# The last retention slot takes the first tile of windowed attention, and the last two retention sequences finish inside the attention slots

## The reference, cut to what matters

```python
# third block, per sequence, 8 heads of 32
qT, kT, vT = proj(Wq), proj(Wk), proj(Wv)
S = g * S + k_t[..., :, None] * v_t[..., None, :]
y_t = jnp.einsum('bhde,bhd->bhe', S, q_t)
out = (ys - mean) * rsqrt(var + EPS)        # mean and var of a head over the sequence
x = layernorm(x + (out * gn_weight + gn_bias) @ Wo.T)
# fourth block, per sequence (depth 2)
h = shift_token(x); q, k, v = split(h @ wqkv)
q, k = rotary_xpos(l2norm(q) * qs, l2norm(k) * ksc)
x = x + local_attention(q, k, v) @ wo       # window of 128 tokens
x = x + (a * gelu(g)) @ w2 + b2
```

## Time and profile before

| | us |
|---|---|
| median of 3 runs (lowest to highest) | 2498.15 (2495.32 to 2499.03) |
| the profiled execution's own time | 2491.8 |
| its span, first to last instruction | 2490.0 |
| PE busy | 2304.1 (93%) |
| DVE / ACT / POOL busy | 1629.3 / 1254.5 / 722.8 |
| mean granted clock of PE | 0.977 of full |

### The profile page before, as it was taken

One profiled execution on the slowest core, in us unless ns is written; L12 is line 12 of the kernel. 1 busy time (PEld: TensorE's weight loads), 2 busy tenths in 40 slices (PEclk: granted clock), 3 DMA queues, 4 the chain that ended last, 5 costly groups with the idle time before them and its releaser, 6 DMA issues.

```text
span 2490.0 us, 42715 instructions
## 1 busy us (share of the span) xinstructions
PE 2304.1 (93%) x16434; PEld 1358.5 (55%) x16434; DVE 1629.3 (65%) x4233; ACT 1254.5 (50%) x2822; POOL 722.8 (29%) x717
## 2 busy tenths in 40 slices
PE   5999999999999899986999999999999999999997
PEld 2333333333552577663656666666666666666664
DVE  5777777776530465654876766677667777777754
ACT  2655555556222352224665566556655655566540
POOL 2222322330120221213433333333333333333321
PEclk7999999999999899988999999999999999999999
DMA  9233333341349301000000000000001000000001
GB/s 296 89 104 102 105 100 110 112 123 43 145 176 420 154 28 67 27 18 28 6 5 2 6 6 5 1 5 31 14 1 52 7 14 19 21 5 22 20 21 37
DMA packets 71114, 158.72 MB, mean 64 GB/s; under 512 B 6352, under 2 KB 48448, under 8 KB 63328
## 3 DMA queue, kind: packets, MB, share of 16 engines
q1 hardware_dynamic: 68608, 146.81, 16.8%
q0 software_dynamic: 2304, 9.18, 1.6%
HBM read 116.65 MB, written 35.13 MB: 61 GB/s over the span
## 4 chain that ended last, share of the span: by engine, by line
PE 72%; DVE 15%; ACT 4%; DMA 3%; issue 2%; POOL 2%; SPq 1%; POOLq 0%; DVEq 0%; ACTq 0%
PE banks L1895 9%; PE banks L1873 6%; PE banks L1754 6%; PE banks L262 5%; PE banks L1768 4%; PE banks L225 4%; PE banks L238 4%; PE banks L1855 3%; PE banks L1798 3%; PE banks L311 2%; PE banks L292 2%; PE banks L1813 2%; DVE arena L2404 2%; DMA arena<-in_e_Wg 2%; PE banks L1780 2%
## 5 line engine op out<-in xcount | busy, mean ns | idle before, releaser
L466 DVE TENSOR_REDUCE arena<-banks 128x1 f32<-128x512 f32 x512 | 324.2, 683 | 113.7 <-PE banks L225 113.6
L381 ACT ACTIVATE arena<-banks 128x512 f32<-128x512 f32 x512 | 279.1, 595 | 164.1 <-PE banks L238 162.2
L1895 PE MATMUL banks<-arena 128*128 128x512 f32 x640 | 293.3, 595 | 6.3 <-DVE arena L2112 5.9
L1965 ACT ACTIVATE arena<-arena 128x256 f32<-128x256 f32 (+1 forms) x512 | 286.4, 562 | 3.5 <-DVE arena L2065 3.1
L2203 POOL TENSOR_TENSOR arena<-arena 128x512 f32<-128x512 f32 x128 | 162.6, 1271 | 401.7 <-DVE arena L2096 401.7
L1754 PE MATMUL banks<-arena 128*128 128x512 f32 x512 | 245.5, 603 | 5.7 <-DVE arena L2096 4.9
L225 PE MATMUL banks<-arena 96*128 96x512 bf16 x512 | 204.2, 401 | 16.6 <-DVE arena L466 12.0
L238 PE MATMUL banks<-arena 128*128 128x512 bf16 x512 | 194.1, 385 | 2.2 <-ACT arena L381 1.3
L2199 POOL TENSOR_TENSOR arena<-arena 128x16 f32<-128x16 f32 x64 | 187.4, 2929 | 5.3
L1895 PEld LDWEIGHTS banks<-arena 128*128 128x128 f32 x640 | 116.8, 190 | 131.6 <-issue 119.4
L1937 ACT ACTIVATE arena<-arena 128x256 f32<-128x256 f32 (+1 forms) x256 | 102.1, 471 | 154.6 <-DVE arena L2041 154.6
(11 more groups left out here) (300 smaller groups left out, 4363.1 us busy)
## 6 DMA issues: line engine op xcount, KB each, us to landing
arena<-in_e_W SPq DMA_DIRECT2D x32, 1024.0 KB, 12.3
arena<-stacks SPq DMA_DIRECT2D x64, 384.0 KB, 4.6
arena<-in_e_Wg SPq DMA_DIRECT2D x16, 1024.0 KB, 14.9
stacks<-arena SPq DMA_DIRECT2D x32, 384.0 KB, 2.5
stacks<-arena SPq DMA_DIRECT2D x32, 256.0 KB, 2.7
arena<-dens POOLq DMA_DIRECT2D x32, 256.0 KB, 4.6
arena<-in_xT SPq DMA_DIRECT2D x8, 512.0 KB, 9.0
stacks<-arena SPq DMA_DIRECT2D x32, 128.0 KB, 2.5
```

The source lines that it names most:

```text
L381: e.activation(ex[:, j], self.psum[:, self.exp_bank1(k)], ACT.Exp).then_inc(s["a_e"], 1)
L466: e.tensor_reduce(mx[:, t, j:j + 1], self.psum[:, k % 3], AX.X, ALU.max, negate=True).then_inc(s["a_m"], 1)
L1895: i = e.matmul(bank, weights[:, c], self.hT[:, c], start=c == 0, stop=c == 1)
L1965: k = e.activation(pr[:, h, at:], pr[:, h, at:], ACT.Exp, bias=mx[:, h:h + 1], scale=rn[:, h:h + 1], accum_out=den[:, h:h + 1])
```

## The change

Slots 9 and 10 of retention and slot 0 of the fourth block are gone as slots of their own. What they held is spread out. The last retention slot (`*3_last`, sequence 7's products) now also has tile 0's projection, squares, lengths, rotation, scaling and values. Slot 1 of the fourth block also has sequence 7's coefficients, head scaling, output product and addition, and sequence 6's statistics and norm. Slot 2 also has the turn of sequence 6 and the statistics, norm and turn of sequence 7. No instruction is added or removed other than waits. `Ring` banks of the last turns are fixed by hand (banks 3 and 5), `out` of sequence 7 uses bank 5 twice. The even and odd buffers of `qk3`, `kn3` and `vn3` change places, so that sequence 7's lie where tile 0's buffers don't, and `state3`, `st3` and `norm3` are placed elsewhere for the same reason.

```diff
+    def tensor3_last(self, e, w):
+        b = SEQS - 1
+        self.tensor3_own(e, w, b, 0)
+        w.wait_ge("r_xTb", SEQS - 3)
+        w.wait_ge("r_xTa", SEQS - 3)
+        self.tensor4_project(e, w, 0, 0)
+        self.tensor3_state(e, w, b, 0)
+        self.tensor3_state(e, w, b, 1)
+        self.tensor4_project(e, w, 0, 1)
+        self.tensor3_y(e, w, b, 0)
+        self.tensor3_own(e, w, b, 1)
+        self.tensor3_y(e, w, b, 1)
+        w.wait_ge("r_a", 8 * SEQS)
+        self.tensor3_turn(e, w, b - 2, 0)
+        self.tensor3_out(e, w, b - 1, 0)
+        self.tensor3_stat(e, w, b)
+        self.tensor3_turn(e, w, b - 2, 1)
+        self.tensor3_out(e, w, b - 1, 1)
+        w.wait_ge("r_mean", SEQS)
+        self.tensor4_values(e, w, 0)
...
     def scalar3(self, e, w):
...
+        b = SEQS - 1
+        self.scalar3_norm(e, w, b - 2)
+        self.scalar4_squares(e, w, 0)
+        self.scalar3_heads(e, w, b - 1)
+        self.scalar3_turn(e, w, b - 2, 0)
+        self.scalar3_turn(e, w, b - 2, 1)
+        self.scalar4_values(e, w, 0)
...
     def vector3(self, e, w):
...
+        self.vector3_stats(e, w, b - 2)
+        self.vector3_own(e, w, b, 0)
+        self.vector3_state(e, w, b, 0)
+        self.vector3_state(e, w, b, 1)
+        self.vector3_coefficients(e, w, b - 1)
+        self.vector4_lengths(e, w, 0)
+        self.vector3_sums(e, w, b, 0)
+        self.vector3_own(e, w, b, 1)
+        self.vector4_rotate(e, w, 0, 0)
+        self.vector3_sums(e, w, b, 1)
+        self.vector4_rotate(e, w, 0, 1)
+        self.vector3_mean(e, w, b)
+        self.vector3_add(e, w, b - 1, 0)
+        self.vector3_add(e, w, b - 1, 1)
+        self.vector4_scale(e, w, 0)
...
     def gpsimd3(self, e, w):
...
+            self.gpsimd3_state(e, w, b, 0)
+            self.gpsimd3_state(e, w, b, 1)
+            if n == SEQS:
+                self.gpsimd4_rotary(e, w, 0)
+                self.gpsimd4_tile(e, w, 0)
+            self.gpsimd3_rsqrt(e, w, b)
...
     def tensor4(self, e, w):
-        for n in range(SLOTS4):
+        for n in range(1, SLOTS4):
             a, b, c, d = (k if 0 <= k < TILES4 else None for k in (n, n - 1, n - 2, n - 3))
             if a is not None:
                 self.tensor4_project(e, w, a, 0)
+            if n == 1:
+                w.wait_ge("r_xTa", SEQS - 2)
+                w.wait_ge("r_x", 2 * SEQS - 2)
+            elif n == 2:
+                self.tensor3_turn(e, w, SEQS - 2, 0)
             if b is not None:
                 self.tensor4_turn(e, w, b, 0)
             if a is not None:
                 self.tensor4_project(e, w, a, 1)
+            if n == 2:
+                self.tensor3_turn(e, w, SEQS - 2, 1)
             if b is not None:
                 self.tensor4_turn(e, w, b, 1)
             self.tensor4_mlp(e, w, n, 1)
+            if n == 1:
+                self.tensor3_out(e, w, SEQS - 1, 0)
...
             if b is not None:
                 self.tensor4_scores(e, w, b)
+            if n == 1:
+                self.tensor3_out(e, w, SEQS - 1, 1)
+            elif n == 2:
+                self.tensor3_turn(e, w, SEQS - 1, 0)
             if a is not None:
                 self.tensor4_values(e, w, a)
+            if n == 2:
+                self.tensor3_turn(e, w, SEQS - 1, 1)
...
     def scalar4(self, e, w):
-        for n in range(SLOTS4):
+        for n in range(1, SLOTS4):
...
+            if n == 1:
+                self.scalar3_heads(e, w, SEQS - 1)
             if c is not None:
                 self.scalar4_divide(e, w, c)
+            if n == 2:
+                self.scalar3_turn(e, w, SEQS - 2, 0)
             if b is not None:
                 self.scalar4_queries(e, w, b)
             if a is not None:
                 self.scalar4_squares(e, w, a)
+            if n == 1:
+                self.scalar3_norm(e, w, SEQS - 2)
+            elif n == 2:
+                self.scalar3_turn(e, w, SEQS - 2, 1)
+                self.scalar3_norm(e, w, SEQS - 1)
+                self.scalar3_turn(e, w, SEQS - 1, 0)
...
             if a is not None:
                 self.scalar4_values(e, w, a)
+            if n == 2:
+                self.scalar3_turn(e, w, SEQS - 1, 1)
             if b is not None:
                 self.scalar4_exp(e, w, b, 0)
...
     def vector4(self, e, w):
...
+            if n == 1:
+                self.vector3_stats(e, w, SEQS - 2)
+                self.vector3_coefficients(e, w, SEQS - 1)
+            elif n == 2:
+                self.vector3_stats(e, w, SEQS - 1)
             if c is not None:
                 self.vector4_divide(e, w, c)
...
     def sync4(self, e, w):
...
         w.wait_ge("t_rotary", 2)
+        w.wait_ge("r_coef", SEQS)
         e.dma_start(self.rot[1], d["rot1"]).then_inc(s["l_rot"], 16)
```

More of the change, by code:

```diff
@@ L1300, in tensor3, with turn_bank3 @@
     def tensor3(self, e, w):
-        for n in range(1, SLOTS3):
+        for n in range(1, SEQS):
             self.tensor3_slot(e, w, n)
+        self.tensor3_last(e, w)
+    def tensor3_last(self, e, w):
[18 more added lines that the diff above has]
+        self.tensor4_values(e, w, 0)
+    def turn_bank3(self, b, c):
+        if b < SEQS - 3:
+            return self.ring3.bank(("turn%d" % c, b, 0))
+        return 3 if b == SEQS - 3 else 5
     def tensor3_slot(self, e, w, n):
@@ L1458, in scalar3_slot @@
         if d is not None:
[L1459 to L1463, removed]
-        if c is not None:
[L1465 to L1469, removed]
+            self.scalar3_norm(e, w, d)
+        if c is not None:
+            self.scalar3_heads(e, w, c)
         if a is not None:
@@ L1479, in scalar3_slot, with vector3_stats, vector3_add @@
         if d is not None:
[L1480 to L1482 removed]
+            self.scalar3_turn(e, w, d, 0)
+            self.scalar3_turn(e, w, d, 1)
     def vector3(self, e, w):
[L1487 removed]
+        for n in range(1, SEQS):
             self.vector3_slot(e, w, n)
+        b = SEQS - 1
+        self.vector3_stats(e, w, b - 2)
[13 more added lines that the diff above has]
+        self.vector4_scale(e, w, 0)
+    def vector3_stats(self, e, w, b):
+        self.stats_of(e, w, "r_x", [2 * b + 1, 2 * b + 1, 2 * b + 2, 2 * b + 2], self.norm3[b % 2], self.x_nat[:, b], self.s["r_sn"])
+    def vector3_add(self, e, w, b, pair):
+        x, bank = self.x_nat[:, b, 2 * pair:2 * pair + 2], 5 if b == SEQS - 1 else 4 + pair
+        w.wait_ge("r_wo", 2 * b + pair + 1)
+        e.tensor_tensor(x, x, split(self.psum[:, bank], 2, CH), ALU.add).then_inc(self.s["r_x"], 1)
     def vector3_slot(self, e, w, n):
@@ L1513, in vector3_slot @@
         if c is not None:
[L1514 to L1517, removed]
+            self.vector3_add(e, w, c, 0)
+            self.vector3_add(e, w, c, 1)
     def vector3_decay(self, e, w, kind, b, g):
@@ L2012, in vector4 @@
                 self.vector4_sums(e, w, d)
+            if n == 1:
+                self.vector3_add(e, w, SEQS - 1, 0)
             if b is not None:
@@ L2184, in gpsimd4 @@
     def gpsimd4(self, e, w):
-        s, own = self.s, self.ownp1
-        self.gpsimd4_rotary(e, w, 0)
-        for n in range(SLOTS4):
+        for n in range(1, SLOTS4):
+            if n <= 2:
+                self.gpsimd3_norm(e, w, SEQS - 3 + n)
             if n == TILES4 // 2 - 3:
```

120 lines of the change are left out of this document (75 added, 45 removed).

## The result

The changed kernel takes 2466.44 us (median of 4 runs, 2463.97 to 2469.19), against 2498.1 us: a ratio of 0.9875, 95% interval 0.9858 to 0.9892. Forecast were 2471.4 us and a gain of 26.8; the medians are 31.7 apart. In three further comparisons of the same two kernels the ratio was 0.9887, 0.9883 and 0.9898 (28.2, 29.2 and 25.5 us of 2498). The four ratios average 28.5 us.

What follows compares the result with a forecast made beforehand. PE, busy 93% of the span, loses time only idle or at lower clock; mid-kernel, engine-to-engine latency binds. -31.2 + 0.4 - 0.1 + 4.1 + 0 = -26.8 us from 2498.15 gives 2471.4; range 2465 to 2482.

Steps and rivals of the forecast that it cites:

- The removed stretch and the merged slot: Retention slots 9, 10 and fourth-block slot 0 go, 31.2 us; sequence 7's slot, with tile 0 added, ends at 1121.9.
- The term of +0.4: Last retention slot, with tile 0's work added, ends at 1121.9 us against 1121.54 before.
- Slot 1: Fourth block: 11.2 us against 11.3, as 3.5 us of added output product fill PE's waits.
- Slot 2: Fourth block: PE waits behind ACT's exponentials, division and copy; 15.9 us, +4.1, bounded by 0 and 8.2.
- rival 1: More low clock at the seam: two more 6.8 us stretches cost 3.4 each; 20.0 us gained, 2478.2 us; 18%.
- Slot 3: Fourth block: nothing added, left at 14.1 us, ending at 1163.1.
- DMA and the hidden work: SP's second rotary table load moves from 1141.39 to about 1144, no cost; tile 0's work on other engines is hidden.
- The function tables: ACT in the mixed slots: no table loads from mixing the blocks, nothing charged.
- rival 3: ACT's path: four table loads of 1283 ns add 5.1 us, giving 2476.5 us; 3%.
- Rival 4: Sequences 6 and 7's turns still wait 6.66 and 6.65 us for norms, now in slot 2; gain 13.5, 2484.7 us; 5%.
- Rival 2: ACT stays behind in slot 3 because tile 1's exponentials come later; another 4.1 us, 2475.5 us; 8%.
- Rival 5: Slower: waits in mixed slots keep renewing the low clock, each further slot costing 13.5 us; 2509.7 us; 3%.

Runs made afterwards that it cites:

- v3: Changed kernel with sequence 6's first turn moved to the end of slot 1 on PE, its copy ahead of ACT's exponentials; 2466.95 us, ratio 0.9879.
- v4: v3 with sequence 7's norm behind four of tile 1's exponentials and its two turns in slot 3, ahead of `attend`; 2469.18 us, ratio 0.9885.
- v8: v3 with sequence 7's statistics and root behind tile 2's rotation, norm and first turn later in slot 3, second turn in slot 4; 2465.81 us, ratio 0.9881.
- v1: Changed kernel with the drain of sequences 6 and 7 as its own stage ahead of slot 1, tile 0 still merged; 2482.8 us, ratio 0.9943.
- v2: Changed kernel with tile 0 in its own slot behind the last retention slot, sequences 6 and 7 still finishing in slots 1 and 2; 2478.5 us, ratio 0.9925.

## Why the prediction was right, point by point

**The removed stretch and the merged slot.** Forecast were 31.2 us out and a slot of 25.7 us (1096.17 to 1121.9). Measured are 24.3 us. The last `y` starts 14.4 us after `own`, forecast 14.0. The first stretch of low clock went with its idle, as forecast, and the second stayed, as forecast; but I gave it the 6.8 us of before, and it lasted 3.4. The term of +0.4 is in truth -1.0. That length is not of the change's making alone: the second profile of the kernel before has 3.4 us in the same place.

**Slot 1.** Forecast 11.2 us, measured 11.2, with one wait of 0.33 us at its end. Sequence 7's output product costs nothing, since it fills waits.

**Slot 2.** Forecast 15.9 us, measured 15.6 at full clock and 17.8 with the drop that three of four profiles show. The mechanism is shown: the same wait, released by the same copy, of 2.37 us (I had 2.7). The term left out, 2.2 us, is that this idle may itself drop the clock; only rival 1 spoke of it. The bounds, 0 and 8.2 us on top of 11.8, held it. What I hadn't seen is that the wait is not the bound: v3 took it away and slot 2 gave back 0.5 us. ACT is busy 12.8 of the 15.6 us in slot 2, against 8.6 of 11.8 before, and has three short waits, 1.0 us for DVE, 0.8 and 1.1 for PE. It takes work out of ACT's list to shorten the slot: v4 left sequence 7's statistics and root in it and came to 13.5 us, with ACT busy for 10.9; v8 took these from DVE and POOL too, with ACT busy for the same 10.9, and came to 13.2.

**Slot 3.** Left at 14.1, measured 13.5. The 14.1 held a stretch of low clock; of the profiles of before, the third has none there and takes 13.4.

**The sum** of the four, 24.3 + 11.2 + 17.8 + 13.5, is 66.9 us against a forecast 66.9 (1096.17 to 1163.1). That it was right to 0.1 us is luck: 1.4 us too many in the merged slot and 0.6 in slot 3 stand against 1.9 too few in slot 2, and all three are in the main the clock. Without the drop in slot 2, as in the second profile, it is 2.2 us too high. The mechanism, two idles of 6.66 us and a slot less against a longer slot 2, doesn't hang on that. The forecast time, 2471.4 us, is 5.0 above the median; beyond these 2.2 us that is spread outside the seam.

**DMA and the hidden work.** SP's second table load came at 1144.29, 1144 forecast. POOL's table preparation ran at 1105.02 and its power at 1107.94; the root for sequence 7 waited 0.31 us for DVE's variance, so this root, the one that could have been late, was not.

**The function tables.** Neither profile has a table load between 960 and 1200 us, and the loads ahead of exponentials are 28 again, as in the earlier trace rows; the squares, norms, copies and exponentials of the mixed slots share a set. The Trainium skill's remark that identity and copy lie in every set (ScalarE: Activation LUTs, "Table sets: the hidden batching unit") agrees, and rival 3 is out.

**The rivals.** Rival 4 (the chain is only moved) is refuted by the missing waits of 6.66 us, and v1, where the chain is moved only to a stage of its own, shows the size of such a cost, 13.0 us by the medians and 14.6 to 16.9 by the seam. Rival 2 is out, slot 3 being shorter than before. Rival 1 happened in part, with one stretch more in slot 2 in three of four profiles, but one of half length in the merged slot. Rival 5 is out: in the seam of the changed kernel the clock came back within 7 us each time. The median is 1.4 us inside the lower end of the range.

## What to carry to other kernels

Where two pipelines meet on the same engines, the last slots of one and the first slots of the other are mostly latency, and each can be laid over the other: here 93.7 us became 66.9, with the overlapped drain worth some 16 and the overlapped fill some 10 to 12 alone. When work is moved into another stage's slots, count it on the engine whose ordered list is fullest, not on the one that waits: removing the visible wait gave 0.5 us, and taking 1.9 us of ACT's busy time out of the slot as well gave 1.7 more (v4), or 2.0 with DVE's and POOL's part (v8). In both the next slot took some back, 3.2 and 1.0 us, so compare at a point two slots further on. And a helper's last copy that frees a shared buffer belongs ahead of everything that its next user doesn't need, or into a later slot: twice it held up PE by 1.7 and 2.6 us.

## What the runs showed of the hardware that I had not expected

The stretches at the lower clock have no one length. After the same idle of 2.70 us ahead of the second `y` it was 6.8 us in the first profile of the kernel before and in v2, 3.4 in the second profile of the very same kernel before and in all ten profiles with tile 0 in the merged slot, and in the third of before it was part of one stretch of 17.1 us from 1101.0 on. The idle of 2.37 us in slot 2 was followed by a stretch of 6.8 us in three profiles and by none in the fourth, with the same instructions at the same distances. Nor does it take one long idle: in v4 and v8 the clock dropped in slot 3 behind idles of 0.26, 0.28 and 1.29 us, the last longer one (1.92 and 1.67 us) having ended 6.5 us earlier. A forecast can give such an idle a price (here 2.2 us) but not a certainty.

Executions of one kernel differ by 10 us in where the seam begins, most of it by the clock between 800 and 880 us (0.91 and 0.81 granted), with the seam itself the same to 0.4 us. A change of this size is better measured on a stretch between two instructions of the trace than on the whole time.
